# Four transformer layers of a graph network: from rolled layers in blocks that meet to one straight block

## The reference, cut to what matters

```
h = x @ Wn + bn
for l in range(4):
    Q, K, V = h @ WQ[l] + bQ[l], h @ WK[l] + bK[l], h @ WV[l] + bV[l]
    scores = sum(Q[dst] * K[src], -1) / sqrt(128)          # one per edge
    attn = softmax of the scores over the edges of a dst
    messages = segment_sum(attn[:, None] * V[src], dst)
    h = layernorm(h + messages @ WO[l] + bO[l]) * ln_g[l] + ln_b[l]
return h @ Wout + bout                                     # added to x
```

## Time and profile before

| | us |
|---|---|
| median of three runs | 3138.56 |
| profiled execution, its own time | 3144.87 |
| its span, first to last instruction | 3143.0 |
| mean granted TensorE clock, share of full | 0.915 |
| the four layers, first k matmul to the end | 1710.9 to 3143.0 |

### The profile page before, as it was taken

The page is one execution under the profiler, slowest core; times in us unless marked ns, Lnnn a source line. Parts: engine busy times, 40 slices in busy tenths (PEclk is TensorE's granted clock), DMA queues, the critical chain, the costliest instruction groups (busy, mean ns, idle before and its releaser), DMA issues. The chain is left out here.

```text
span 3143.0 us, 60275 instructions
## 1 busy us (share of the span) xinstructions
PE 2562.9 (82%) x19197; PEld 2091.6 (67%) x19197; DVE 2451.5 (78%) x5292; ACT 1962.9 (62%) x3958; POOL 221.3 (7%) x487
## 2 busy tenths in 40 slices
PE   0888878857468888788874899969997899969997
PEld 0555555546346666566653798858895789848886
DVE  7999999834489999899967777667775777657776
ACT  1666666611258888788873677647774577647774
POOL 3000000000000000000000111011110111001110
PEclk9999999978678999889986999989998999989999
DMA  1232332373152335323311333133341333224332
GB/s 41 73 128 90 126 128 108 147 238 109 42 164 103 107 120 163 123 103 109 118 46 68 130 140 143 64 107 127 139 145 42 124 133 135 84 84 144 130 137 59
DMA packets 87373, 355.45 MB, mean 113 GB/s; under 512 B 47453, under 2 KB 59541, under 8 KB 59796
## 3 DMA queue, kind: packets, MB, share of 16 engines
q1 hardware_dynamic: 87149, 352.59, 32.3%
HBM read 285.86 MB, written 65.67 MB: 112 GB/s over the span
## 5 line engine op out<-in xcount | busy, mean ns | idle before, releaser
L1824 ACT ACTIVATE awcol<-l_aturned 125x500 fp32r<-125x500 f32 (+2 forms) x489 | 279.9, 572 | 251.8 <-PE l_aturned L1771 247.8
L1365 PE MATMUL gturned<-ident,grow 125*125 125x125 f32 x2500 | 411.9, 307 | 29.0 <-ACT grow L1303 29.0
L1864 DVE TENSOR_TENSOR awcol<-l_aturned,awcol 125x500 fp32r<-125x500 f32 (+2 forms) x489 | 321.2, 657 | 122.3 <-ACT awcol L1824 119.8
L1365 PEld LDWEIGHTS gturned<-ident,grow 125*125 125x125 f32 x2500 | 334.4, 205 | 107.4 <-issue 72.5
L1272 DVE SCALAR_TENSOR_TENSOR grow<-line,a_dst 125x3125 f32<-125x3125 f32 x100 | 347.6, 3476 | 39.8 <-DMA line<-lines_dram 24.5
L1303 ACT ACTIVATE grow<-grow,neg 125x3125 f32<-125x3125 f32 x100 | 290.4, 2904 | 123.4 <-DVE neg L1284 123.4
L1783 PE MATMUL l_asum<-awcol,vals_high 125*128 125x512 f32 (+1 forms) x975 | 360.9, 391 | 5.6 <-DVE awcol L1864 3.1
L1281 DVE CUSTOM_DVE_ANT_0 grow<-grow,bias 125x3125 f32<-125x3125 f32 x100 | 341.6, 3416 | 25.8 <-DMA bias<-bias_dram 11.5
L1343 PE MATMUL gparts<-gwcol,h_mem 125*32 125x125 f32 x5000 | 245.7, 291 | 114.5 <-ACT gwcol L1316 114.4
L1783 PE MATMUL l_asum<-awcol,vals_low 125*128 125x256 f32 x975 | 304.2, 321 | 3.3 <-DVE awcol L1864 1.2
L1316 ACT ACTIVATE gwcol<-gturned 125x1000 f32<-125x1000 f32 x300 | 282.1, 1002 | 20.3 <-PE gturned L1365 20.3
(11 more groups left out here) (346 smaller groups left out, 5766.1 us busy)
## 6 DMA issues: line engine op xcount, KB each, us to landing
abias<-bias_dram SPq DMA_DIRECT2D x100, 1562.5 KB, 6.5
bias<-bias_dram SPq DMA_DIRECT2D x50, 1562.5 KB, 6.5
bias_dram<-lnrow SPq DMA_DIRECT2D x25, 1562.5 KB, 5.2
counts_dram<-pair SPq DMA_DIRECT2D x13, 1562.5 KB, 6.4
pair<-counts_dram SPq DMA_DIRECT2D x13, 1562.5 KB, 16.4
line<-lines_dram SPq DMA_DIRECT2D x8, 1367.2 KB
fixed<-kp SPq DMA_DIRECT2D x250, 4.0 KB, 1.7
agg<-counts_dram SPq DMA_DIRECT2D x2, 1367.2 KB
```

Of the source, the lines that this page charges most:

```text
L1365: last = pe.transpose(bank[q % RING][:, j // 4, j % 4 * T:(j % 4 + 1) * T], row[n % RING][:, t * T:(t + 1) * T], ident[0:T, 0:T])
L1824: act.activation(operand(P, e, u, 0), turned(P, e, u), ACT.Copy).then_inc(high_copied, 1)
L1864: dve.tensor_tensor(operand(P, e, u, 1), turned(P, e, u), operand(P, e, u, 0).bitcast(FP32), ALU.subtract).then_inc(low_made, 1)
```

## The change

All four layers are written out one behind the other in one single block (`for l in range(LAYERS)` on each engine, with `project(l)`, `attend(l)`, `leave(l)`), and so is the output projection. There is no meeting of the engines between or within layers and no clearing: every semaphore counts on, and each wait has the layer's share added. The bank ring is the three banks of the transposes and one of the two sum banks; k of the next layer waits for the chunk of `cols` that it reads. The inner loop over pairs remains, with four rounds of two pairs in place of five.

Within a layer: PE does k, q, then the first ten chunks of scores, and only then the value rows, and then waits until all of them are read. The value rows go into x in place of `agg`. The single block is block 0, ahead of the twelve pairs: `first` does its 7 chunks and 3 of the next pair, and each of its 7 units does two chunks ahead. ACT does the exponentials of block 0 before the values. SP waits until q and v are all read (`banks.done`) before it issues `load_ahead`, and the bias loads of the layer stand behind that; the first two bias loads of the next layer are issued at the end of the layer before. Only `q{l}` chunk 0 is awaited by POOL for block 0.

```diff
+        banks = Banks([*turned_ps, sum_ps[1]], sem("filled"), {...}, stages)
+        v_whole = x
+        single = lambda P: isinstance(P, int) and P == 0
+        block_of = lambda P, half: 2 * P - 1 + half
+        def over_pairs(eng, step):
+            step(0, 0)
+            step(1, 1)
+            with eng.Fori(0, (LAST_PAIR - 4) // 2) as i:
+                step(2 * i + 2, 0)
+                step(2 * i + 3, 1)
+            for P in range(LAST_PAIR - 2, LAST_PAIR + 1):
+                step(P, P % 2)
+        def ahead(P, e, u, act_on):
+            for k in ((2 * u, 2 * u + 1) if single(P) else (u, u + 1) if u == UNITS - 1 else (u,)):
+                g = k + AHEAD
...
+        def first(act_on, then=AHEAD):
+            for c in range(NC):
+                act_on(0, 0, 1, c)
+            for c in range(then):
+                act_on(1, 1, 0, c)
...
+                for l in range(LAYERS):          # SP
+                    last = l == LAYERS - 1
+                    banks.done(sp, f"q{l}", NC)
+                    banks.done(sp, f"v{l}", NC)
+                    load_ahead(l, last)
+                    def step(b, p):
+                        sp.wait_ge(scores_read, b * NC + (1 + LAYER_CHUNKS * l))
+                        load_bias(b, p)
...
+                    first(scores)                # PE, attend(l)
+                    pe_rows(pe, banks, f"v{l}", [cols], [w[:, 2, :]])
+                    banks.done(pe, f"v{l}", NC)
+                    over_pairs(pe, step)
+                    weigh(LAST_PAIR, 0, UNITS - 1)
...
+                    first(exponential, 0)        # ACT, attend(l)
...
+                        act.activation(vals_high[:, part, :], v_whole[:, part, :], ACT.Copy).then_inc(v_rounded, 1)
+                    over_pairs(act, step)
...
+                    first(maximum)               # DVE, attend(l)
+                    values(l)
+                    over_pairs(dve, step)
...
-                        load_ahead(sp, l, last)
-                        def step(b, p):
-                            sp.wait_ge(scores_read, b * NC + 1)
-                            sp.dma_start(bias[p][:, :], G["bias_dram"][b, :, :]).then_inc(bias_in[p], 16)
...
-                if not last:
-                    with nc.Block() as block:
-                        @block.sync
-                        def _(sp):
-                            for s in kept.values():
-                                sp.sem_clear(s)
-
-        with nc.Fori(0, LAYERS - 1) as l:
-            layer(l, False, "l3")
-        layer(LAYERS - 1, True, "l3_last")
```

More of the change, by code:

```diff
@@ L82, with __init__ @@
 class Norm:
[L86 removed]
+    def __init__(self, sem, name, stat, x, h, spare, relu=True, turn=0):
+        self.turn = turn
         self.scales_ready, self.scalar_done = sem(f"{name}_scales"), sem(f"{name}_scalar")
@@ L1548, in sem @@
             return kept[name]
[L1550 to L1559, removed]
+        ps = lambda name: ctx.enter_context(nc.psum_tensor(name, [128, 512], FP32))
@@ L1561, in load_ahead, with message, _ @@
+        def message(P):
+            return cols[:, 0:T] if single(P) else cols[:, bass.ds(P * (2 * T) - T, 2 * T)]
+        with nc.Block() as block:
+            @block.sync
+            def _(sp):
+                def load_ahead(l, last):
                     sp.dma_start(w[:, 3, :], G["L3_gnn_WO"][l, :, :]).then_inc(loaded, 16)
@@ L1977, in _ @@
                         part = slice(ts[0], ts[-1] + 1)
[L1978 to L1987 removed]
+                        act.wait_ge(v_made, NC * l + c + 1)
@@ new lines, in attend, with leave, evacuate @@
+                        act.activation(vals_high[:, part, :], v_whole[:, part, :], ACT.Copy).then_inc(v_rounded, 1)
+                    over_pairs(act, step)
+                    finish(LAST_PAIR, 0)
+                def leave(l):
+                    norms[l].root(act)
+                    def evacuate(c):
+                        a, z = CHUNKS[c]
+                        bank = banks.full(act, f"normed{l}", c)
+                        act.activation(cols[:, a:z], bank[:, 0:z - a], ACT.Identity, bias=affine[:, 1:2], scale=affine[:, 0:1]
+                                       ).then_inc(banks.read["act"], 1)
+                    act.wait_ge(loaded, ahead_loads(l))
+                    done = 0
+                    for n, t in enumerate(t for t in range(NT) if owner[t] == "act"):
+                        norms[l].tile_by_act(act, t).then_inc(normed["act"], 1)
+                        if n:
+                            evacuate(done)
+                            done += 1
+                    for c in range(done, NC):
+                        evacuate(c)
@@ L1988, in _ @@
                     for c in range(NC):
                         ts = tiles_of(c)
-                        bank = banks.full(dve, "out", c)
-                        here = x[:, ts[0]:ts[-1] + 1, :]
-                        dve.tensor_tensor(here, here, rows_view(bank, c, D), ALU.add).then_inc(banks.read["dve"], 1)
+                        bank = banks.full(dve, f"v{l}", c)
+                        dve.tensor_tensor(v_whole[:, ts[0]:ts[-1] + 1, :], rows_view(bank, c, D),
+                                          rows[:, BV, :].unsqueeze(1).broadcast_to([T, len(ts), D]), ALU.add
+                                          ).then_inc(v_made, 1)
@@ L1995 @@
+                for l in range(LAYERS):
+                    project(l)
+                    attend(l)
+                    leave(l)
+                dve.wait_ge(x_in, LANDED)
+                for c in range(NC):
+                    ts = tiles_of(c)
+                    bank = banks.full(dve, "node_out", c)
+                    here = x[:, ts[0]:ts[-1] + 1, :]
+                    dve.tensor_tensor(here, here, rows_view(bank, c, D), ALU.add).then_inc(banks.read["dve"], 1)
 INPUTS = ["x", "src", "dst",
```

669 lines of the change are left out of this document (313 added, 356 removed).

## The result

The changed kernel takes 3108.0 us (median of five runs, 3098.5 to 3115.1) against 3136.3 for the kernel before beside it: 0.9906 of its time, 95% interval 0.9879 to 0.9933. The forecast was 3112, faster.

What follows compares the result with a forecast made beforehand. PE, busy nearly throughout the pairs, bounds the kernel, so only its waits can be won. Terms -16.5 - 1 - 12.8 + 4 = -26.3 take the profiled 3144.87 to 3118.6, or 3112 against the median 3138.56; range 3092 to 3130.

Steps and rivals of the forecast that it cites:

- Boundaries: Between layers, PE's k follows the last transposes without a meeting, -16.5 us; the other meetings, into last stage and output, -1.
- a rival: At layer boundaries, new code still costs each the 3.23 us of the third; 9 of 16.5 lost, 3121, chance 0.10.
- The clock of k and q: k and q of layers 1 to 3 might start at full clock; none taken, since clock stays 0.50 through the transposes.
- the bound of 7.4: Upper limit, if k and q of layers 1 to 3 lost their 2.1 to 2.8 us excess over layer 0.
- The order inside a layer: Scores ahead of values, single block first: 2.3 us gained a layer, 3.6 more in layer 3; -12.8 us.
- +4 for the clock: Half clock after PE's second idle in each layer's single block, charged 1 us a layer, between 0 and 3.
- -1 for the meetings: Meetings into the last stage of a layer and into the output cost 0.3 us each; -1 us in all.
- the late load: In the single block, block 2's bias load waits behind value rows and small loads, read at 39.4; costs 4.1 us.
- The pairs: From pair 1 to a layer's last message: ten full pairs 231.9, pair 11 21.7, pair 12 shorter; 274.5 us.
- the 15 us: Possible gain from one saved turn of the inner pair loop in each layer; the sum takes nothing.
- The load in time: Bias load lands in time or PE's idle is shorter: 16.4 and the clock's 4 go, 3092; chance 0.15.
- Half clock through the whole single block: Slower rival: PE's 17.2 us of work there takes 34.4, pair 1 at 62.3; 3160, chance 0.08.

Runs made afterwards that it cites:

- the run with the bias load first: Changed kernel with SP issuing block 2's bias load before waiting for the value rows and before the next layer's small loads; 0.9829 of the kernel before.
- the run with the values spread: On top of issuing block 2's bias load first, ACT's rounding and DVE's low part of the value rows go unit by unit into the single block; 0.9770.

## Why the prediction was right, and where it was not

**Boundaries, forecast -16.5 and -1.** Right: the idle of 17.1 us went to nothing. What it was made of was not known then, and a rival took 3.2 us of new code as its fixed part; the runs put a meeting at 1.16 and the turn back at 4.0, and new code at nothing (k follows the transposes without a bracket). Of the other meetings the one into the last stage hardly cost anything (idle of 0.96 us before, 0.92 after), the one into the output 1.0 once.

**The clock of k and q, forecast 0.** This is the term that was missed. k and q of layers 1 to 3 were 2.05, 2.61 and 2.82 us longer than those of layer 0, 7.5 in all; after, k to scores exceeds layer 0's 10.29 by 0.44, 0.31 and 0.42. So 6.3 us came in where the forecast gave the bound of 7.4 and took none. Its reason was that the clock stays at half through the transposes. So it does. But k was slow because of the idle between the transposes and itself: with k right behind them the clock rises 0.7 to 1.0 us into k (in the other runs without this idle from just before k to 2.5 us into it), with 1.16 us of idle only after 3.8 to 4.1, and behind a clock at full and 2.97 us of idle it fell within k. A stretch at half clock ahead says little of the next one; what PE does in between is what counts.

**The order inside a layer, forecast -12.8 and +4 for the clock, so with -1 for the meetings -9.8.** Measured is 30.4 - 17.1 - 6.3 = 7.0. Of this 5.6 lie in layer 3: from its k to the end of the span it was 365.4 and is 357.4, and 2.4 of these 8.0 are k's clock. Layer 3 had 4.9 in the forecast, but for another reason in part: the late load was charged to it as to the others, and it cost 2.9 there in place of 5.1. Layer 0 gained nothing where 2.3 less 1 was forecast, and layers 0 to 2 together 1.4 where it was 3.9. The steps there:
- q's end, the scores right behind it (10.3), the value rows behind these and `load_ahead` at 28.3 (forecast 28.0) came as worked out. PE's idle was 4.31 (5.3).
- The bias load's way from issue to reader was 8.2 us in place of 6.75: mis-sized by 1.5. The 6.75 was a load issued 6 us after the last of the small ones; here it followed them at once. DVE waited 6.30 for it, and pair 1 started at 52.4 in place of 49.2.
- PE's stop of 4.08 was forecast as 4.6, the half clock behind it as 1 us; the difference of stop and whole loss in the run with the bias load first puts it at 1.7.
- The pairs, forecast 274.5, took 2020.94 - 1747.39 = 273.6. By the starts of DVE's last step on a message, a pair takes 23.1 to 23.3 us inside the loop and written out alike; so the turn saved gave nothing, and the 15 us that the prediction weighed and left out were rightly left out.

**The rivals.** The load in time was priced at 16.4 + 4 = 20.4 us; taking the lateness away gave 19.8. So that price was right in all, though not layer by layer (5.8, 6.3, 4.8 and 2.9 where it had 5.1 in each), and it is the size of what the change left lying. Half clock through the whole single block did not come: after its first stop the clock was back within 3.4 us (0.78 at 1723.22, 0.34 at 1726.59).

What no step asked was whether the value rows belong behind the scores at all. The forecast booked the order as a gain with a late load; the runs show that this order causes the lateness and costs 18 us as it stands, and that the single block's place pays it back. The total came out near, -30.4 in the trace where the sum had -26.3, because the clock of k, taken as 0 and worth 6.3, stood against an order that gained 2.8 less. The idle at the boundaries and the late load were rightly seen; that the misses had opposite signs was luck. What x in place of `agg` is worth was not tried by itself.

## What to carry to other kernels

When a step is moved, look at the queue of the engine that issues its loads: what waited for the old place now waits for the new one, and a large load right behind nine small ones was late twice, in issue and in landing. A boundary between unrolled or looped stages is worth its idle time and the half clock behind it. And a long rounding pass whose parts are used one by one should be made part by part, beside the work that uses them.

## What the runs showed of the hardware

- Turning back a hardware loop with a whole layer as its body cost PE 4.0 us (6.9 to 7.0 against 2.96), a meeting of all engines 1.16 us of idle and about 1.6 us of lower clock behind it (12.2 to 12.4 us from k to the first scores in place of 10.6 to 10.7).
- A bias load of 1562.5 KB landed in 6.5 to 6.8 us when issued ahead of nine small loads, and in 8.0 to 8.4 right behind them; right behind four small ones in 6.4. Why it does was not tried further.
- Behind transposes at half clock the granted clock was at full from between 0.1 us ahead of k and 2.5 us into it, where k followed at once; with 1.16 us of idle between, from 3.8 to 4.1 us into k. A stop of 0.99 us at full clock, in the run with the values spread, left it at full.
- Equal code ahead of the transformer took 1692 to 1713 us in eleven profiled executions, the one of the kernel before among them. For an edit behind it the interval inside the trace tells more than the span: it repeated within 0.7 us, though single layers of it moved by 1.9 and 2.5.
